# Reordering the first window of a fused text and image cross-attention kernel

## The reference

```python
q = heads(hidden_states @ W_q)                       # x: [16, 128, 160]
k_t, v_t = heads(text @ W_k), heads(text @ W_v)      # text: [16, 124, 256]
probs_t = softmax(q @ k_t^T * scale)
text_out = probs_t @ v_t
k_ip, v_ip = heads(ip @ W_k_ip), heads(ip @ W_v_ip)  # ip: [16, 4, 256]
qsem = l2norm(probs_t @ text)                        # per head, 256 wide
sem = qsem @ l2norm(ip)^T
probs_ip = softmax(q @ k_ip^T * scale + 0.5 * sem) * spatial_mask
out = (text_out + probs_ip @ v_ip) @ W_out + b_out + hidden_states
```

## Time and profile before

| | |
|---|---|
| median of 3 runs | 218.13 us (216.04, 218.13, 218.46) |
| profiled execution: time, span from first to last instruction | 217.86 us, 215.8 us |
| busy: PE, DVE, ACT, POOL | 204.6, 181.1, 169.1, 149.7 us |
| granted TensorE clock, mean of the span | 1.000 |

### The profile page before, as it was taken

One profiled execution on the slowest core, in us unless ns is written; L12 is line 12 of the kernel. 1 busy time (PEld: TensorE's weight loads), 2 busy tenths in 40 slices (PEclk: granted clock), 3 DMA queues, 4 the chain that ended last, 5 costly groups with the idle time before them and its releaser, 6 DMA issues.

```text
span 215.8 us, 6904 instructions
## 1 busy us (share of the span) xinstructions
PE 204.6 (95%) x1589; PEld 191.5 (89%) x1589; DVE 181.1 (84%) x1147; ACT 169.1 (78%) x554; POOL 149.7 (69%) x255
## 2 busy tenths in 40 slices
PE   8898959999997999999999999999999999998984
PEld 8777959999996999999999999999999999987973
DVE  4547758998977798997979797989979798989893
ACT  2639949897986888897988888888969888887721
POOL 2165007379794979879696969698796969697870
PEclk9999999999999999999999999999999999999999
DMA  5524443837364462747365554647364656433101
GB/s 132 146 83 105 109 122 64 225 77 237 58 174 122 120 185 56 208 109 210 95 186 122 163 140 130 170 88 213 68 205 100 189 120 171 94 92 103 46 5 46
DMA packets 41580, 27.45 MB, mean 127 GB/s; under 512 B 8513, under 2 KB 39898, under 8 KB 41562
## 3 DMA queue, kind: packets, MB, share of 16 engines
q1 hardware_dynamic: 40922, 26.81, 47.5%
q10 hardware_dynamic: 640, 0.43, 0.8%
HBM read 10.06 MB, written 1.43 MB: 53 GB/s over the span
## 4 chain that ended last, share of the span: by engine, by line
PE 77%; DVE 5%; POOL 4%; DMA 4%; SPq 4%; ACT 3%; issue 2%; POOLq 0%; DVEq 0%
PE main_ps L974 14%; PE main_ps L976 14%; PE probsT_ps L956 13%; PE pa L946 9%; PE score_ps L1010 7%; DMA k_split<-kip_d 4%; PE pb L1038 4%; PE pb L1050 3%; PE pa L1066 3%; SPq L385 2%; PE main_ps L891 2%; PE pa L1058 2%; POOL rnorm L511 2%; PE pa L886 2%; DVE junk L734 2%
## 5 line engine op out<-in xcount | busy, mean ns | idle before, releaser
L629 ACT ACTIVATE probs<-score_ps,negmax 128x124 f32<-128x124 f32 x320 | 92.5, 401 | 2.0 <-DVE negmax L799 1.9
L734 DVE CUSTOM_DVE_ANT_0 junk<-main_ps,probs 128x124 f32<-128x124 f32 x320 | 77.8, 280 | 2.3 <-PE main_ps L976 2.1
L974 PE MATMUL main_ps<-main_rhs,probsT 124*128 124x137 f32 x320 | 64.2, 281 | 0.7 <-DVE small L736 0.6
L976 PE MATMUL main_ps<-main_rhs,probsT 124*128 124x137 f32 x320 | 63.3, 279 | 0.0
L511 POOL TENSOR_TENSOR rnorm<-clamped,exponent 128x20 f32<-128x20 f32 x15 | 53.2, 3545 | 1.1 <-DVE clamped L719 1.1
L799 DVE TENSOR_REDUCE negmax<-score_ps 128x4 f32<-128x496 f32 x80 | 53.1, 663 | 0.0
L597 ACT ACTIVATE probsT<-probsT_ps 124x512 f32<-124x512 f32 x80 | 49.8, 622 | 3.4 <-PE probsT_ps L956 3.2
L974 PEld LDWEIGHTS main_ps<-main_rhs,probsT 124*128 124x128 f32 x320 | 49.0, 190 | 1.7 <-issue 1.3
L976 PEld LDWEIGHTS main_ps<-main_rhs,probsT 124*128 124x128 f32 x320 | 48.7, 188 | 0.0
L956 PE MATMUL probsT_ps<-ident_sb,probs 128*124 128x128 f32 x320 | 47.9, 272 | 0.0
L956 PEld LDWEIGHTS probsT_ps<-ident_sb,probs 128*124 128x124 f32 x320 | 38.4, 139 | 5.9
(11 more groups left out here) (162 smaller groups left out, 319.2 us busy)
## 6 DMA issues: line engine op xcount, KB each, us to landing
main_rhs<-g_stage SPq DMA_DIRECT2D x16, 660.0 KB, 4.1
vrep<-vip_d SPq DMA_DIRECT2D x13, 320.0 KB, 3.5
k_diag<-k_stack SPq DMA_DIRECT2D x60, 48.0 KB, 2.2
ctxT_sb<-ctxT SPq DMA_DIRECT2D x16, 124.0 KB, 2.7
k_diag<-k_stack SPq DMA_DIRECT2D x60, 32.0 KB, 2.0
xT_sb<-xT SPq DMA_DIRECT2D x16, 80.0 KB, 2.1
xn_sb<-xn SPq DMA_DIRECT2D x15, 80.0 KB, 2.0
out<-out_sb SPq DMA_DIRECT2D x15, 80.0 KB, 3.5
```

The lines of the kernel that those rows point to most:

```text
L629: last = act.activation(probs[p][:, h, :], score_ps[(p * G + g) % 2][:, j * TOK:j * TOK + T], ACT.Exp, bias=negmax[p][:, h:h + 1])
L734: dve.tensor_tensor_reduce(junk[:, 2 * r + a, :], u, probs[wb][:, h, :], 1.0, 0.0, ALU.mult, ALU.add, norm2[wb][:, h:h + 1])
L974: pe.matmul(main_ps[r][:, 0:MAIN], probsT[mp][:, 2 * r, :], blk[:, RW - MAIN:RW], start=True, stop=True)
L976: pe.matmul(main_ps[r][:, MAIN:2 * MAIN], probsT[mp][:, 2 * r + 1, :], blk[:, 0:MAIN], start=True, stop=True).then_inc(s_main, 1)
```

## The change

All of it lies in the prologue and in window 0; windows 1 to 15 have the same instructions in the same order.

- **Blocks of group 0 first.** ACT and DVE copy only the group 0 part (128 columns) of turned K to `k_diag[0]` before the first score. ACT then copies `q_stack`, and the blocks of groups 1 to 3 (384 columns) follow. Group 4 and the last `q_stack` block come after the first group's softmax (`first_rest` on ACT and DVE). DVE computes `ipunit` ahead of the low half of q.
- **G and V of batch 0** move behind the first score on PE, into the banks `main_ps[1]` and `main_ps[0]`.
- **Image keys.** The projection of image keys and values (`project_ip`, 12 matmuls) moves from the prologue to the end of group 3 of window 0, into the bank `pb`; the four DVE copies that read it move from group 2 to group 4, ahead of `norms`. The fifth q turn of batch 1 waits until they are done. On SP the two writes to `kip_d` and `vip_d` move behind all eight `k_diag` blocks and ahead of the broadcast.
- **Early clear.** POOL clears `k_diag[1]` near its start, not after the V columns of batch 0.
- **Batch 1's turns** and the ACT and DVE work on them stand one group later in window 0: K turns in group 2, q turns in group 3. ACT's `gkv_stages` follow the exponentials of group 1, and `k_stacked` those of group 2.

The diff, cut to its core:

```diff
@@ SP, window 0
                     for odd in range(2):
-                        if odd == 1 and w == 0:
-                            sp.wait_ge(s_kip, 2)
-                            sp.dma_start(kip_d, kip_split[...]).then_inc(s_kip_out, 16)
                         for j in range(HG):
...
+                    if w == 0:
+                        sp.wait_ge(s_kip, 2)
+                        sp.dma_start(kip_d, kip_split[...]).then_inc(s_kip_out, 16)
+                        sp.wait_ge(s_vip, 1)
+                        sp.dma_start(vip_d, vip_sb[:, :]).then_inc(s_vip_out, 16)
                     wait(sp, s_main, NPAIR * b)
                     wait(sp, s_gstage, b + 2)
                     sp.dma_start(main_rhs[n][:, :, D + 1:D + 1 + NIP + TOK], ...)
-                    if w == 0:
-                        sp.wait_ge(s_vip, 1)
-                        sp.dma_start(vip_d, vip_sb[:, :]).then_inc(s_vip_out, 16)
@@ POOL
+            pool.memset(k_diag[1][:, :, :, :].bitcast(F32), 0.0).then_inc(s_zeros[1], 1)
             pool.memset(oT[:, :, :], 1.0).then_inc(s_fill, 1)
...
             v_columns(0)
-            pool.memset(k_diag[1][:, :, :, :].bitcast(F32), 0.0).then_inc(s_zeros[1], 1)
@@ ACT, prologue
-                last = act.activation(k_diag[0][rows, j, 0:G - 1, :], pa[rows, :]..., ACT.Copy)
+                act.activation(k_diag[0][rows, j, 0, :], pa[rows, 0:TOK], ACT.Copy).then_inc(s_kd0_0, 1)
             act.wait_ge(s_qT, 1)
             act.activation(q_stack[0][:, 0:G - 1, :]..., main_ps[1][:, :], ACT.Copy).then_inc(s_qst03, 1)
+                last = act.activation(k_diag[0][rows, j, 1:G - 1, :], pa[rows, TOK:]..., ACT.Copy)
+            act.wait_ge(s_g0_mm, 1)
+            act.activation(g_stage[0][:, NIP:NIP + TOK], main_ps[1][:, 0:TOK], ACT.Copy)
...
+            def first_rest():
+                act.wait_ge(s_ctx_mm, 1)
+                act.activation(v_stage[:, :], main_ps[0][0:T, 0:C], ACT.Copy).then_inc(s_v0, 1)
+                act.wait_ge(s_kq4, 1)
+                for j in range(2):
+                    act.activation(k_diag[0][rows, j, G - 1, :], pb[rows, 0:TOK], ACT.Copy).then_inc(s_kd0_4, 1)
@@ ACT, window 0
                     if g == 0 and w == 0:
+                        first_rest()
+                    if g == 1 and w == 0:
                         gkv_stages(b, p, i, w)
-                    if g == 1 and w == 0:
+                    if g == 2 and w == 0:
                         k_stacked(b, p, i)
@@ DVE, prologue and window 0
+            def first_rest():
+                dve.wait_ge(s_kq4, 1)
+                for j in range(2, HG):
+                    dve.tensor_copy(k_diag[0][rows, j, G - 1, :], pb[rows, 0:TOK]).then_inc(s_kd0_4, 1)
+                dve.wait_ge(s_kd0_4, HG)
+                dve.tensor_copy(q_stack[0][:, G - 1, :], pb[:, TOK:TOK + S]).then_inc(s_st4, 1)
...
-                    if g == 2 and w == 0:
+                    if g == 4 and w == 0:
                         dve.wait_ge(s_vipT_mm, 1)
-                        kips = by_head(main_ps[0][0:B * NIP, 0:C])
+                        kips = by_head(pb[0:B * NIP, C:2 * C])
@@ PE, window 0
                     if g == 0 and w == 0:
+                        pe.wait_ge(s_ipcol, 1)
+                        project(main_ps[1][:, 0:TOK], ctxT_sb[0], ...).then_inc(s_g0_mm, 1)
+                        pe.wait_ge(s_wv_in, 16)
+                        project(main_ps[0][:, 0:C], ctxT_sb[0], ...).then_inc(s_ctx_mm, 1)
...
+                    if g == 3 and w == 0:
+                        project_ip()
+                    if g == 4 and w == 0:
+                        pe.wait_ge(s_vipT, 1)
+                        turn_q_last(b)
```

More of the change, by code:

```diff
@@ L565, in _ @@
                            ACT.Copy).then_inc(s_qst03, 1)
[L566 to L570, removed]
+            for j in range(2):
+                rows = slice(32 * j, 32 * j + 32)
+                last = act.activation(k_diag[0][rows, j, 1:G - 1, :],
+                                      pa[rows, TOK:].rearrange("r (g t) -> r g t", t=TOK), ACT.Copy)
+                if j == 0:
+                    last.then_inc(s_kd0_03, 1)
+                else:
+                    last.then_inc(s_kst03, 1)
+            act.wait_ge(s_g0_mm, 1)
+            act.activation(g_stage[0][:, NIP:NIP + TOK], main_ps[1][:, 0:TOK], ACT.Copy)
+            act.activation(g_stage[0][:, 0:NIP], main_ps[1][:, T:TOK], ACT.Copy).then_inc(s_gstage, 1)
+            def first_rest():
+                act.wait_ge(s_ctx_mm, 1)
+                act.activation(v_stage[:, :], main_ps[0][0:T, 0:C], ACT.Copy).then_inc(s_v0, 1)
+                act.wait_ge(s_kq4, 1)
+                for j in range(2):
+                    rows = slice(32 * j, 32 * j + 32)
+                    act.activation(k_diag[0][rows, j, G - 1, :], pb[rows, 0:TOK], ACT.Copy).then_inc(s_kd0_4, 1)
             def gkv_stages(b, p, i, w):
@@ L591, in k_stacked, with q_stacked, q_stacked_last @@
                                ACT.Copy).then_inc(s_kst03, 1)
+            def q_stacked(b, n):
+                wait(act, s_qT, b + 2)
+                act.activation(q_stack[n][:, 0:G - 1, :].rearrange("r g t -> r (g t)"), pa[:, :],
+                               ACT.Copy).then_inc(s_qst03, 1)
+            def q_stacked_last(b, n):
+                wait(act, s_kq4, b + 2)
+                act.activation(q_stack[n][:, G - 1, :], pb[:, TOK:TOK + S], ACT.Copy).then_inc(s_st4, 1)
             def transposed(t, tp):
@@ L605, in window @@
                         gkv_stages(b, p, i, w)
[L606 to L614, removed]
+                    if g == 3 and has(w) and has(w, ahead=1) and w != 0:
+                        q_stacked(b, n)
+                    if g == 4 and has(w) and has(w, ahead=1) and w != 0:
+                        q_stacked_last(b, n)
                     if has_group(w, g, 2):
@@ L692, in _ @@
                 rows = slice(32 * j, 32 * j + 32)
[L693 to L698, removed]
+                dve.tensor_copy(k_diag[0][rows, j, 0, :], pa[rows, 0:TOK]).then_inc(s_kd0_0, 1)
             dve.wait_ge(s_ipunit_T, 1)
@@ L741, in window @@
                     grp = b * G + g
-                    if g == 2 and has(w, ahead=1):
+                    if g == (3 if w == 0 else 2) and has(w, ahead=1):
                         wait(dve, s_qhi, b + 2)
@@ L800, in window @@
                                           negate=True).then_inc(s_max, 1)
-                    if g == (1 if w == 0 else 0) and has(w, ahead=1):
+                    if g == 0 and w == 0:
+                        first_rest()
+                    if g == (2 if w == 0 else 0) and has(w, ahead=1):
                         wait(dve, s_khi, b + 2)
@@ L915, in _ @@
             mm.then_inc(s_qT, 1)
+            pe.matmul(pb[:, TOK:TOK + S], stacked(q_split, G - 1), ident_r_sb[:, :], start=True, stop=True).then_inc(s_kq4, 1)
             pe.wait_ge(s_ident_in, 16)
@@ L947, in project_gkv, with turn_q_last @@
                 mm.then_inc(s_ctx_mm, 1)
+            def turn_q_last(b):
+                wait(pe, s_final, b - 2)
+                wait(pe, s_qlo, b + 2)
+                pe.matmul(pb[:, TOK:TOK + S], stacked(q_split, G - 1), ident_r_sb[:, :], start=True,
+                          stop=True).then_inc(s_kq4, 1)
             def transposes(b, p, g):
@@ L1051, in window @@
                         mm.then_inc(s_q_mm, 1)
-                    if g == 1 and has(w, ahead=1):
+                    if g == (2 if w == 0 else 1) and has(w, ahead=1):
                         wait(pe, s_klo, b + 2)
```

98 lines of the change are left out of this document (44 added, 54 removed).

## The result

The changed kernel took 218.23 us in the median of 20 runs (216.79 to 219.75), the kernel before 217.06 in 20 runs beside it (215.93 to 218.97). The ratio is 1.0052, with a 95% interval of 1.0028 to 1.0075: 1.1 us slower, within 1%. The profiled execution has a span of 217.0 us and a mean granted clock of 0.988.

What follows compares the result with a forecast made beforehand. PE was taken to bound the kernel, held in window 1 by the load from `kip_d`. 217.86 + 0.2 = 218.1, or 218.3 from the median of before; 218.2 us was taken, range 216.4 to 220.0.

Steps and rivals of the forecast that it cites:

- Parts 1 to 4: Prologue and window 0: first score 2.7 us earlier, 2.5 left at second exponentials, then spent; `k_stack` ends at 19.1, 0.3 later.
- Part 5: SP's queue behind `k_stack`: eleven DMAs, load issued at 26.6; PE goes on in window 1 at 30.65, 0.2 us later.
- the two ends given: Load's landing after the broadcast's issue: at most 4.73 us in the 85 us window, 5.7 in window 1 of before; 4.7 taken.
- The rival that the broadcast delays the load: Window 1: the image rows come at 31.5, the kernel is 1.1 us slower at 219.3; chance 22%.
- its mark of 31.2: Window 1: K turns starting above 31.2 us would show the broadcast delaying the load.
- Part 6: PE's arrival at window 1's K turns: second `mains` 1.2 to 1.6 us later, arrival 29.4 to 29.8, hidden by the load wait.
- if that cover were gone, it is what the change gives: Window 1: without the load wait, PE's arrival 0.6 to 1.0 us before 30.42 would be the change's gain.
- The shift stays to the end: After 30.42 us all instructions are the same, so the 0.2 us shift lasts to the kernel's end.
- one of the signs of being wrong: Whole kernel: wrong if ACT doesn't set `k_stack`, PE no longer waits for the load, or a new wait appears after 31 us.

Runs made afterwards that it cites:

- the load first: Window 1's load from `kip_d` issued ahead of batch 1's broadcast: changed kernel 215.99 us; kernel before 214.24, and 214.55 on a second chip.
- `k_stack` earlier: Changed kernel with ACT's `k_stack` copy ahead of the third group's exponentials in window 0: 216.71 us, ratio 0.9984 to the kernel before.
- SP's order alone: Kernel before with only the writes to `kip_d` and `vip_d` moved behind all eight `k_diag` pieces, ahead of the broadcast: 218.15 us, ratio 1.0020.

## Why the prediction was right

Each step in the two profiles of the changed kernel:

| step (us) | predicted | first | second |
|---|---|---|---|
| first score starts | 10.0 | 10.69 | 9.94 |
| second exponentials end | 15.9 | 16.49 | 15.75 |
| `k_stack` ends | 19.1 | 19.33 | 18.57 |
| image keys there | 22.1 | 23.37 | 22.28 |
| eight pieces end, `kip_d` issued | 24.3 | 25.41 | 23.88 |
| load issued | 26.6 | 27.56 | 26.04 |
| load lands, after the broadcast's issue | 4.7 | 4.96 | 5.11 |
| PE arrives | 29.4 to 29.8 | 30.60 | 29.52 |
| PE goes on | 30.65 | 31.78 | 30.41 |

**Parts 1 to 4.** The mechanism is as predicted. The head start of 2.0 to 2.7 at the first score is used up by waits on ACT and DVE and by the work now ahead of `k_stack`, which ends 0.5 later than before in one profile and 0.2 earlier in the other. The sums lie between the two. Most of their distance is there before any reordered step of PE or DVE: PE's 20 warm-up matmuls take 4.63 in the first and 3.95 in the second, and DVE starts K's low half at 8.05 and 7.16. In the kernel before the same matmuls took 4.24 and, with the load first on the second chip, 4.63. So this is a scatter of every version, and no cost of the change. One term stands clear of it: from the end of the second exponentials to that of `k_stack` the sum had 3.2, and both profiles have 2.84 and 2.82. The stages and the `probsT` copy took 0.96 and 0.47 of the chain in the first, not 1.08 and 0.60.

**Part 5.** SP had no pause for the image keys, 2.0 ahead in the first profile and 1.6 in the second. In the first, PE went on 1.1 later than predicted: `k_stack` 0.2, the pieces 0.9 (6.08 against 5.2, one issue of 1.46 among them), the two writes 0.2 less, the landing 0.3 more. The landing after the broadcast was sized too short: 4.7, measured 4.96 and 5.11. It lies between the two ends given, 4.73 and 5.7, though the same order on the kernel before had 4.38. Too short by 0.3 to 0.4 here, too long by 0.4 up to `k_stack` and by 0.2 at the two writes: these errors largely cancel in the 30.65. (`project_ip` is 8 matmuls in the kernel, 16 in the trace, not 12; the 1.90 taken for it is not touched by that.) The rival that the broadcast delays the load had the right mechanism and too high a price; its mark of 31.2 was passed in the first profile, but by the long issue and the late start.

**The order of the ring.** The rows of SP agree with the ordered ring that the Trainium skill describes (page "DMA: Bandwidth & Descriptors", section "Queues, rings and completion order"): close behind the broadcast the load took 3.46, 4.08 and 4.23, ahead of it 2.33 at most. The 2.0 of the section "Anatomy of one DMA", which is headed for DMAs that GpSimd issues and not SP, fits only the load that stands ahead of the broadcast.

**Part 6.** `mains` waits 0.91 for `norms`, at 24.02 against 23.1 to 23.5 predicted, and 22.93 in the second profile. The wait for the load hid this, as said. What I said of the cover is wrong in its sign: "if that cover were gone, it is what the change gives". With the load first the changed kernel is not faster than the kernel before with the same edit, but 1.75 slower (215.99 against 214.24, on one chip). I had compared PE's new arrival with the time of the load; against PE's old arrival of 28.21 it is a loss of 2.4 in the first profile and 1.3 in the second, on either side of the 1.75.

**After window 1.** "The shift stays to the end" is only roughly so. The same load makes PE wait again in window 2 or 4: 1.36 at 66.20 before, 0.95 at 67.37 in the first profile, 0.63 at 42.19 in the second. The last is a wait after 31 us that was not there before, one of the signs of being wrong that I had named; it is the same load in another window, and the first profile doesn't have it. From the K turns of window 1 to the end are 185.4, 185.2 and 184.7; in the seven profiles without a load wait after window 1 it is 183.6 to 184.0.

**The size.** The median of 218.23 hits the 218.2, but in part by luck: the base was 218.13 from three runs, and 20 runs put it at 217.06. The change costs 1.1, where the sum had 0.1 to 0.2. Which part does it is open. With `k_stack` earlier some of it seems to go; SP's order alone shows 0.2% and the early clear 0.1%, neither clear of zero. Part of it goes with the clock: beside the second profile, the runs of 0.995 or more have 217.12 (7 runs) against 216.59 of the kernel before (16 runs), 0.5 apart. The two profiles of the changed kernel go on 1.36 later and 0.01 earlier than the one of before, so they can't divide it.

## What to carry to other kernels

Find the wait that ends last in the stage and follow it through the DMA queue before counting a gain upstream: here 2.0 to 2.7 us at the first score vanished behind eleven DMAs, one of them a broadcast of 660 KB. Here a load of 5 KB that an engine waited for belonged ahead of the large transfer on its queue; look for such a pair. Where a wait hides a change, compare the engine's own arrival before and after too, since a hidden loss comes out as soon as the wait is mended.

## What was not expected of the hardware

**Long DMA issues.** An issue that mostly takes SP 0.6 now and then takes 1.2 to 1.6, and not always the same one: before it was the load, 1.24 at 26.27; with the load moved ahead it was the next DMA in that place, 1.33 at 26.26; in the changed kernel it was the third `k_diag` piece, 1.46 at 20.73, as with SP's order alone (1.62). Ahead of the load such an issue goes straight into its time. No run explains it.

**The clock.** In the first profile of the changed kernel TensorE's granted clock was at half, that is at 1.2 GHz, from 10.5 to 13.9 us, while the second kept 2.4. It fell in PE's pause of 0.4 ahead of the first score; the second profile has the same pause and no fall. Windows of both (stretch, length, busy us per engine, granted clock, DMA share, GB/s), the first profile and then the second:

```profile
10.60:13.60 3.00, 2.91 (x10) 2.80 (x11) 2.47 (x7) 2.04 (x8) 0.19 (x1) 0.50 0.00 0
```

```profile
10.60:13.60 3.00, 3.00 (x24) 2.92 (x22) 1.79 (x5) 2.10 (x10) 0.52 (x3) 1.00 0.32 96
```

PE executed 10 matmuls in the one and 24 in the other, and the first score took 0.77 instead of 0.47. Yet the second exponentials end 0.74 later in the first profile, no more than the 0.75 by which the first score was already late. Four of the changed kernel's 20 runs held the full clock throughout and took 217.3, 218.0, 219.0 and 219.27. So the low clock is not what set window 1 in this pair, and a full clock alone doesn't bring the changed kernel to the 217.06 of before. But over many runs clock and time go together. Of the 69 runs of the kernel before beside the experiments, 18 had a mean granted clock of 0.992 or less, and on the chip that has 13 of them these took 1.5 us longer than the others (218.15 against 216.59). There is no profile of such a run of the kernel before, so where it loses the time stays open.
